# First-loop passes of the expert part by a stage table for each engine

## What is computed

```python
for _ in range(2):
    z_norm = rmsnorm(z, norm_w)                    # z starts as layernorm(x)
    scores = softmax(z_norm @ router_w)            # 8 experts
    topk_vals, topk_idx = top_k(scores, 2)
    topk_vals = topk_vals / (sum(topk_vals) + 1e-9)
    cw = sum(one_hot(topk_idx) * topk_vals)
    mixed = sum over e of cw[:, e] * ((silu(z_norm @ w1[e]) * (z_norm @ w3[e])) @ w2[e])
    z = z + mixed
return x + z
```

## Time and profile before

| | us |
|---|---|
| median of 3 runs (2240.65 to 2243.47) | 2240.81 |
| the profiled execution | 2240.62 |
| its span | 2238.8 |
| expert part: first table operation to the span's end | 1563.1 to 2238.8 |
| tile 0's x transpose | 1584.2 |
| tile 76's | 1748.0 |
| tile 318's | 2193.3 |

### The profile page before, as it was taken

How to read it: one execution, slowest core, us unless ns; L and a number is a source line. 1 busy time by engine, 2 the same in 40 slices (tenths; PEclk the granted TensorE clock), 3 DMA queues, 4 the chain that set the end, 5 groups by cost and what they waited for, 6 DMA issues and landing times. The chain is left out here.

```text
span 2238.8 us, 47085 instructions
## 1 busy us (share of the span) xinstructions
PE 1989.0 (89%) x14589; PEld 951.3 (42%) x14589; DVE 1827.6 (82%) x5158; ACT 1467.0 (66%) x3369; POOL 1234.4 (55%) x1708
## 2 busy tenths in 40 slices
PE   5999999999998899889999999997688999999993
PEld 1222222222222366444444444443355666666662
DVE  8899999999999576788888888888677777767555
ACT  1788888888888623477777777773455655565551
POOL 6253343334321002476767677754767777777776
PEclk9999999999999999799999999997799999999996
DMA  7345335444542002234242433322233444444544
GB/s 188 106 118 144 110 105 139 137 105 122 144 106 87 11 1 57 58 69 106 59 113 61 100 75 87 87 60 64 83 108 112 123 121 119 121 127 124 145 136 114
DMA packets 224625, 226.92 MB, mean 101 GB/s; under 512 B 34049, under 2 KB 187521, under 8 KB 224385
## 3 DMA queue, kind: packets, MB, share of 16 engines
q1 hardware_dynamic: 152432, 164.62, 28.5%
q0 software_dynamic: 16384, 33.59, 5.3%
q10 hardware_dynamic: 55568, 25.71, 4.1%
HBM read 96.48 MB, written 125.76 MB: 99 GB/s over the span
## 5 line engine op out<-in xcount | busy, mean ns | idle before, releaser
L937 ACT ACTIVATE big<-mid_ps 128x512 f32<-128x512 f32 (+2 forms) x1792 | 914.2, 568 | 266.1 <-PE mid_ps L816 258.4
L1022 DVE TENSOR_REDUCE mid_nmax<-mid_ps 128x1 f32<-128x512 f32 (+2 forms) x1280 | 776.4, 657 | 61.3 <-PE mid_ps L795 36.2
L795 PE MATMUL mid_ps<-KT,QT 48*128 48x512 bf16 (+3 forms) x2048 | 604.4, 351 | 68.2 <-DVE mid_nmax L1022 49.6
L816 PE MATMUL mid_ps<-QT,KT 64*128 64x512 bf16 (+3 forms) x2048 | 563.9, 346 | 2.6 <-ACT big L937 2.2
L832 PE MATMUL mid_ps<-big,vv 128*32 128x512 f32 (+3 forms) x4096 | 466.7, 529 | 17.0 <-POOL big L1153 13.3
L795 PEld LDWEIGHTS mid_ps<-KT,QT 48*128 48x128 bf16 x2048 | 158.9, 94 | 585.1 <-DVE mid_nmax L1022 397.3
L1019 DVE CUSTOM_DVE_ANT_0 big<-mid_ps,mask 128x512 bf16<-128x512 f32 (+1 forms) x512 | 304.4, 619 | 68.5 <-PE mid_ps L795 63.7
L1666 PE MATMUL moe_ps<-big,moe_xinT 128*128 x638 | 332.1, 602 | 0.0
L1811 POOL DMA_INDIRECT moe_yg<-rows_out,moe_gat_idx x256 | 250.1, 977 | 85.9 <-issue 65.7
L1797 POOL DMA_INDIRECT rows_in<-moe_xn,moe_scat_idx x240 | 236.2, 984 | 81.2 <-issue 61.3
L1839 DVE TENSOR_TENSOR moe_h<-moe_ps,moe_sg 128x256 f32<-128x256 f32 x319 | 135.0, 423 | 157.3 <-ACT moe_sg L1737 152.6
(11 more groups left out here) (359 smaller groups left out, 3017.7 us busy)
## 6 DMA issues: line engine op xcount, KB each, us to landing
l_spread<-mid_slots SPq DMA_DIRECT2D x128, 384.0 KB, 5.3
rows_in<-mid_blank SPq DMA_DIRECT2D x64, 512.0 KB, 4.4
QT<-l_spread SPq DMA_DIRECT2D x128, 192.0 KB, 4.3
KT<-l_spread SPq DMA_DIRECT2D x128, 192.0 KB, 5.3
moe_xin<-rows_in SPq DMA_DIRECT2D x319, 64.0 KB
rows_out<-moe_y ACTq DMA_DIRECT2D x319, 64.0 KB
x<-in_L_attn_x_dram SPq DMA_DIRECT2D x8, 512.0 KB, 6.9
QT<-mid_mrows SPq DMA_DIRECT2D x256, 6.0 KB
```

The costliest lines, as they stand in the source:

```text
L795: mm = pe.matmul(ps[:, bank, n_keys * a:n_keys * (a + 1)], QT[rows, par, pair, i * P:(i + 1) * P], KT[rows, par, pair, 0:n_keys], start=Tr ...
L816: mm = pe.matmul(ps[:, bank, m * a:m * (a + 1)], KT[rows, own, pair, i * P:(i + 1) * P], QT[rows, own, pair, SEQ - m:SEQ], start=True, sto ...
L937: act.activation(weights_of(r, i, heads), ps[:, ring(S2, n - 2, k), 0:widths[i] * len(heads)], ACT.Exp, scale=scale).then_inc(exp_done, 1)
L1022: dve.tensor_reduce(to, of, X_AXIS, ALU.max, negate=True).then_inc(s1_used, 1)
```

## The change

- `tile_of(k, s, behind)` takes the place of the formula. For passes 1 to 6 (`made(k)`) it reads `AHEAD`, a table for each engine with the distance of each stage from `begin[k]`; tables (s from 21) start 10 steps behind `begin` and go two parts to a step. A stage can't be set ahead of an engine's loop 0. The other passes keep the formula, but ScalarE's stages 5 and 6 of passes 7 to 15 come one loop later.
- `begin` changes for passes 2 to 7 and 9: 2 from -1 to -2, 3 from 8 to 7, 4 from 22 to 18, 5 from 34 to 33, 6 from 46 to 44, 7 from 60 to 56, 9 from 97 to 98.
- The tables of unit 0 (eight parts) are made behind VectorE's stage 5 of pass 1, so behind its z, instead of ahead of everything.
- In `transfers` g8 moves behind s4, and g9 behind s7. Scatters of pass 1 are ready at -8 instead of 0, which lets the first three go without a wait.

Worked out for the passes 2 to 6 with b = `begin[k]`, in loops of each engine:

| stage | before | after |
|---|---|---|
| VectorE z (4) | b+1 | b |
| TensorE transposes (5, 6) | b+4, b+4 | b+2, b+3 |
| ScalarE copies (5, 6) | b+3, b+3 | b+2, b+3 |
| TensorE logits, lT (8, 10) | b+5, b+6 | b+4, b+5 |
| VectorE xn (9, 10) | b+4, b+4 | b+2, b+3 |
| VectorE 12; 13, 14; 15 | b+5; b+6; b+7 | b+5; b+6; b+7 |
| ScalarE exp (15) | b+8 | b+7 |
| TensorE K (16) | b+9 | b+8 |
| VectorE 17, 18 | b+8 | b+9 |
| VectorE 19, 20 | b+9 | b+8 |
| VectorE tables (21 to 28) | b+10 to b+13 | b+10 to b+13 |

```diff
--- before.py
+++ after.py
@@ -1439,18 +1439,31 @@
     HT, MOST = IT * max(sizes), max(tiles_in)
     unit_of = [max(u for u in range(UNITS) if first_of[u] <= k) for k in range(LOOPS * GROUPS)]
     EARLY, PER_TILE = 2, 0.5
-    begin = {2: -1, 3: 8, 4: 22, 5: 34, 6: 46, 7: 60, 8: 76, 9: 97, 10: 117, 11: 137, 12: 158, 13: 179, 14: 200, 15: 224,
+    begin = {2: -2, 3: 7, 4: 18, 5: 33, 6: 44, 7: 56, 8: 76, 9: 98, 10: 117, 11: 137, 12: 158, 13: 179, 14: 200, 15: 224,
              16: 256, 17: 270, 18: 286, 19: 308, 20: 325}
-    transfers = ("s1 s2 s3 g8 s4 s5 s6 g9 s7 g10 s8 g11 s9 g12 s10 g13 s11 g14 s12 g15 s13 g16 s14 g17 s15 g18 "
+    transfers = ("s1 s2 s3 s4 g8 s5 s6 s7 g9 g10 s8 g11 s9 g12 s10 g13 s11 g14 s12 g15 s13 g16 s14 g17 s15 g18 "
                  "g19 g20 g21 g22 g23").split()
 
     def length(k):
 
-        return 10 if k < GROUPS - 1 else 14 if k < GROUPS else 20 if k < LOOPS * GROUPS else 8
-
-    def sides(n):
-
-        return [(k, s) for k, at in begin.items() for s in range(STAGES + TABLES) if at + s * length(k) // STAGES == n]
+        return 14 if k < GROUPS else 20 if k < LOOPS * GROUPS else 8
+
+    ON_PE, ON_ACT, ON_DVE = 2, 1, 0
+    AHEAD = {ON_PE: {5: 0, 6: 1, 8: 2, 10: 3, 16: 6}, ON_ACT: {5: 1, 6: 2, 9: 3, 15: 6},
+             ON_DVE: {4: 0, 9: 2, 10: 3, 12: 5, 13: 6, 14: 6, 15: 7, 19: 8, 20: 8, 17: 9, 18: 9}}
+
+    def tile_of(k, s, behind):
+
+        if made(k) and s < STAGES:
+            return max(begin[k] + AHEAD[behind].get(s, 0), -behind)
+        if made(k):
+            return begin[k] + 10 + (s - STAGES) // 2
+        late = 1 if behind == ON_ACT and s in (5, 6) and routes(k) else 0
+        return begin[k] + s * length(k) // STAGES + late
+
+    def sides(n, behind):
+
+        return [(k, s) for k in begin for s in range(STAGES + TABLES) if tile_of(k, s, behind) == n - behind]
 
     def assigned():
 
@@ -1458,7 +1471,7 @@
         for name in transfers:
             k = int(name[1:])
             if name[0] == "s":
-                ready += [0 if k < EARLY else begin[k] + (STAGES - 1) * length(k) // STAGES + 1] * (2 * IT)
+                ready += [-IT if k < EARLY else tile_of(k, STAGES - 1, ON_DVE) + 1] * (2 * IT)
                 due_at += [base_of[unit_of[k]] - RING] * (2 * IT)
             else:
                 ready += [base_of[unit_of[k - GROUPS] + 1] + LAG + 1] * (2 * IT)
@@ -1472,6 +1485,10 @@
             latest = min(latest, due_at[i])
             spread[i] = min(spread[i], latest)
         return spread
+
+    def made(k):
+
+        return 1 <= k < GROUPS - 1
 
     def routes(k):
 
@@ -1603,7 +1620,7 @@
                     side(k, s)
             for n in range(N + LAG + 1 + behind):
                 tile(n)
-                for k, s in sides(n - behind):
+                for k, s in sides(n, behind):
                     side(k, s)
             for k in range(EARLY + len(begin), SIDES):
                 for s in range(STAGES + TABLES):
@@ -1907,7 +1924,7 @@
                         moments()
                         c.link(dve.tensor_tensor(ms[:, :], mean[:, :], mean[:, :], ALU.mult))
                         c.link(dve.scalar_tensor_tensor(var[:, :], var[:, :], 1e-6, ms[:, :], ALU.add, ALU.add))
-                elif 1 <= k < GROUPS - 1:
+                elif made(k):
                     own = slice(IT * (k - 1), IT * k)
                     if s == 4:
                         c.link(dve.tensor_tensor(zs, xs, each_row(lead.means[:, own]), ALU.subtract))
@@ -1933,17 +1950,19 @@
                     if s == 5:
                         c.link(dve.tensor_tensor(var[:, :], var[:, :], rstd[:, :], ALU.mult))
                         c.link(dve.tensor_scalar(var[:, :], var[:, :], 1e-6, None, ALU.add))
+                if (k, s) == (1, 5):
+                    for part in range(TABLES):
+                        make_tables(0, part)
                 if not routes(k):
                     return
 
-                made = 1 <= k < GROUPS - 1
-                scale = lead.scales[:, IT * (k - 1):IT * k] if made else rstd[:, :]
-                if s == 6 and not made:
+                scale = lead.scales[:, IT * (k - 1):IT * k] if made(k) else rstd[:, :]
+                if s == 6 and not made(k):
                     rsqrt_seed(c, rstd[:, :], var[:, :])
                     cubic_root(c, rstd[:, :], var[:, :], tmp[:, :])
-                if s == 7 and not made:
+                if s == 7 and not made(k):
                     cubic_step(c, rstd[:, :], tmp[:, :])
-                if s == 8 and not made:
+                if s == 8 and not made(k):
                     c.link(newton(c, rstd[:, :], var[:, :], tmp[:, :]))
                 if s in (9, 10):
                     if s == 9 and k >= 3:
@@ -2053,8 +2072,6 @@
                     else:
                         c.link(last)
 
-            for part in range(TABLES):
-                make_tables(0, part)
             run(tile, side, 0)
```

## The result

The changed kernel takes 2258.52 us (2256.32 to 2259.77), the kernel before 2241.56 beside it (2240.65 to 2243.95): a ratio of 1.0072, 95% interval 1.0059 to 1.0085. It is slower, by about 17 us. The forecast of 2241.9 was wrong, and the time lies far outside 2234 to 2247. The profiled execution has a span of 2257.2 us.

A forecast was written before the change was run, and what follows sets the result against it. TensorE, busy 89% of the span, was taken as the bound, made late mostly by VectorE. Terms +1.9 + 1.1 - 2.5 + 1.2 - 0.6 = +1.1 on the median 2240.81 gave 2241.9 us; range 2234 to 2247.

The forecast's parts named there:

- ScalarE's later copies: Second loop, passes 7 to 15: zT copied one loop later, behind the activations, bank free by 0.2 us; priced at nothing.
- late copies: Rival, second loop: the later copies miss by more than 0.2 us, some 0.5 a pass, +4.5, 2246; chance 0.07.
- K of passes 4 to 6: First loop: TensorE's counts wait 1.65 us for VectorE's selb; net +0.66 a pass, +1.9 for the three.
- z wait: First loop: TensorE's first transposes wait 0.9 us for VectorE's z, offset by -0.93 from splitting the transposes; together nothing.
- Tiles 0 to 20: First loop, passes 2 and 3, walked stage by stage: +1.1 us, the least trusted term, between -3 and +4.
- Tables of unit 2 and z of pass 5: First loop: table parts in loops 28 to 31 and z in loop 33 make TensorE lose less; -2.5 us.
- Unit 3's tables and pass 7: First loop, from T(53): VectorE's side work shares five loops, from 54 to 58, instead of seven; +1.2 us.
- Pass 9 at 98: Second loop: one loop between tables and adds gives VectorE up to 1.06 us more; taken as -0.6.
- T(0): Start of tile 0's x transpose, 1584.18 us before; claimed to stay at 1584.2, as it follows SP's first load.
- the rival (2247): First loop: the waits in loops 6, 9 and 15 drop TensorE's clock, likely +5, at most +7.8; chance 0.14.
- the Trainium skill's rule: First loop: short matmul bursts between waits are throttled anew, so each of three waits costs 2.6 us; 2249.
- Shorter distances suffice: Rival, first loop: VectorE is ready earlier, so no waits for K or z; about -7, 2235; chance 0.22.

The follow-up runs named there:

- b3: The kernel before with only ScalarE's stages 5 and 6 of passes 7 to 15 one loop later; 2252.92 us, ratio 1.0053.
- a2: The changed kernel with only ScalarE's stages 5 and 6 of passes 7 to 15 one loop earlier again; 2245.75 us, ratio 1.0019.
- c3: The changed kernel with ScalarE's later copies kept in their loop but set ahead of its store of y; 2246.9 us, ratio 1.0024.
- k1: a2 with TensorE's and ScalarE's stages of passes 2 to 6 one loop later, VectorE's 17 to 20 reordered, pass 7 at 60, pass 9 at 97; 2240.31 us.
- m2: k1 with GpSimd's gathers of pass 9 ahead of the scatters of pass 7 again; 2233.1 us, ratio 0.9965.
- d: a2 with only TensorE's and ScalarE's stages of passes 2 to 6 one loop later; only disturbed runs, 2534.05 to 2544.21 us.
- n: a2 with pass 9's gathers ahead of pass 7's scatters; only disturbed runs, 2530.2 and 2530.08 us, ratios 1.0013 and 1.0019.

## Why the prediction was wrong, step by step

**The step that failed** is the one on ScalarE's later copies, "The copy then ends at T + 1.95 and PE asks for the bank at T + 2.18: free by 0.2", priced at nothing. The term was worth +10.9 by itself (b3) and +13.1 in the changed kernel (311.3 less 298.2 in a2), where the lower clock behind pass 9's wait came on top. Two things were wrong with it. I put the copy behind "the activations" and forgot what else ScalarE's loop issues: the store, with its wait for VectorE's y. And I priced it at nothing with a margin of 0.2, the smallest of the whole working, times eight passes. Without the store the step would have been nearly right (1.3 in all in c3). Its rival stood there, "late copies", with the right sign and place, at 0.5 a pass and 0.07. The price of a miss was taken too low, since the copy was thought to be late by tenths, and not bound to another engine's instruction.

**The first loop** came out as worked out, in kind and nearly in size: 2.8 instead of 1.7. Part of that closeness is luck, as 1.5 of the 2.8 is a drop of the clock that the sum didn't have and that a2's execution of the same tiles hadn't at that place (see the clock below); tiles 0 to 76 took 0.8 more than before in a2.
- *K of passes 4 to 6*: forecast 1.65 of waiting. Measured, pass 4, here in loop 26: T(26) to T(27) takes 3.60 instead of the 1.63 of a free loop.

```profile
1647.32 0.21 PE L1730 MATMUL moe_ps<-moe_selb,lead_upper 128*128 128x72 bf16 x1 [1.52 <-DVE moe_selb L1991]
```

- *z wait*: forecast 0.9 for each of passes 4 to 6; 2.6 in 3 waits from 1620 to 1700 us (a2's row above).
- *Tiles 0 to 20*: forecast +1.1, measured +1.8. The three waits that I forecast in loops 6, 9 and 15 came, with 1.99, 2.40 and 2.42 instead of 2.0, 2.4 and 2.7:

```profile
1599.77 0.21 PE L1730 MATMUL moe_ps<-moe_selb,lead_upper 128*128 128x72 bf16 x1 [1.99 <-DVE moe_selb L1991]
...
1607.07 0.66 PE L1712 MATMUL moe_ps<-ident,big 128*128 128x128 f32 x4 [2.40 <-DVE big L1931]
...
1622.90 0.21 PE L1730 MATMUL moe_ps<-moe_selb,lead_upper 128*128 128x72 bf16 x1 [2.42 <-DVE moe_selb L1991]
```

- *Tables of unit 2 and z of pass 5*: forecast -2.5. T(35) to T(39) shrinks by 4.0 (13.57 in rows 3, now 9.58). The tables now lie ahead of it, in loops 28 to 31, in a stretch (T(20) to T(35)) that also has pass 4's K and grew by 2.4. Together -1.6, where the terms for pass 4 (+0.6) and these give -1.9.
- *Passes 5 and 6*, T(39) to T(53): +1.6, forecast 1.3. *Unit 3's tables and pass 7*, T(53) to T(76): +0.9, forecast +1.2.
- *Pass 9 at 98*: forecast -0.6. a2 has -1.1 and -0.6 in tiles 95 to 102 and 108 to 116, but +0.5 and +1.4 in 102 to 108 and 116 to 123: +0.2.

**T(0)** was to stay at 1584.2 and is 1585.81. The last scatter of pass 0 is issued 0.76 later (1579.60 less 1578.84), as the whole part starts later in that execution; over the seven kernels of the table it is issued between 1578.1 and 1579.6. The other 0.98 is new: the scatter takes 1.94 instead of 0.96, beside VectorE's z of pass 2, which the change moved there:

```profile
1579.46 1.23 DVE L1930 TENSOR_TENSOR big<-x,lead_means 128x1024 f32<-128x1024 f32 x1
1579.60 1.94 POOL L615 DMA_INDIRECT rows_in<-lead_xn,lead_scat  x1 [0.30 <-DVE moe_scat_idx L2013]
...
1583.88 11.42 SPq L1646 DMA_DIRECT2D moe_xin<-rows_in  x11
```

The same issue takes 1.94 in all five kernels with z at that place (after, a2, c3, k1, m2) and 0.96 to 0.97 in the two without it (before, b3). That VectorE's operations make it long is read from this overlap; no run changes that alone. The Trainium skill, GPSIMD Engine Reference, "Key points", says that GpSimd shares its interfaces to SBUF with VectorE and suffers from VectorE's instructions with two SBUF inputs; both operations here have two, and the trace agrees.

**The clock.** I gave 0.14 to the three waits dropping it. In this execution one of the three did: behind the 2.42 of loop 15 two gate matmuls take 1.91 instead of 1.02, at a granted clock of 0.50 (1.2 GHz). The others kept it, and over the 20 tiles the mean is 0.89 against 0.86, as the 3.21 gap of before with its own drop is gone. The length of a wait doesn't decide it. In a2, with the same instructions in these tiles, the 1.95 of loop 6 is followed by the lower clock (0.50 from 1601 to 1603 us), which the z wait of loop 9 then absorbs (0.80 instead of 2.40), and the 2.42 of loop 15 isn't; in c3 both are. T(15) to T(17) takes 7.80 here and 6.13 in a2, so a drop cost 1.7 there, not my 2.6. Two more that I had not named stand in pass 7's part, behind 3.47 us of waiting for y, and behind pass 9's wait for `moe_zT` (the row in b3's section). The stretch behind loop 6's wait, with loop 9's in it, the one behind loop 15's, and the one in pass 7's part (busy time of PE, PEld, DVE, ACT, POOL, then the granted clock), and the wait itself:

```profile
1600.00:1612.00 12.00, 9.61 (x66) 6.35 (x62) 10.06 (x33) 6.73 (x19) 9.14 (x9) 1.00 0.30 87
1624.00:1626.00 2.00, 2.00 (x6) 1.15 (x5) 1.80 (x8) 0.03 (x1) 0.97 (x1) 0.50 0.23 72
1718.00:1722.00 4.00, 3.62 (x12) 2.23 (x12) 3.50 (x17) 1.77 (x6) 3.09 (x4) 0.61 0.26 79
```

```profile
1717.84 0.44 PE L1676 MATMUL moe_ps<-ident,moe_h 128*128 128x128 f32 x2 [3.47 <-DVE moe_y L1865]
```

So the rival (2247) did not come true, though a part of it did. Nor did what I made of the Trainium skill's rule, that every one of the three costs its 2.6 (by the forecast's own sum 2249.7, where I wrote 2249). The case in the Trainium skill, TensorE: Matmul & The Clock Gate, "HAM oscillation — how this bites in real kernels", has waits that are longer than the bursts of matmuls between them. Here the waits of 2.0 to 2.4 stand some 5 and 13 us of work apart, so the rule was stretched.

**"Shorter distances suffice"** (0.22, 2235) was wrong in its mechanism, as the waits show, and couldn't have given 2235 either. With tiles 5.5 us earlier than before, k1 has the same span, as GpSimd's queue is full. The sentence on the queue, "Nothing waits, and what is queued behind them on GpSimd keeps its due steps", failed as well: the scatters of pass 7 wait 9.9 us for their indices in the kernel after, and its queue is 5 us behind from there. In the kernel after that is hidden by the 11.59 at the third-last group, and so wasn't part of the 17 us; in k1 the same idle time took back the whole gain of the tiles.

**Still open** is what each part of k1's edit is worth: TensorE's later stages, pass 7 back at 60, pass 9 back at 97 (d was to tell), and what the order of the transfers is worth in a2 (n). From k1 to m2 it was 7.3 us of span.

## What to carry to other kernels

Before an instruction is moved on an in-order engine, write down everything that this engine issues in the loop, its DMA issues and their waits included, and find who ends the last wait ahead of the new place; a margin of tenths is no cover, and it counts once for every pass. When tiles get earlier and the end doesn't, look for a queue that never pauses, and at its last idle time: from k1 to m2 that went from 9.6 to 2.8 us, and the span was 7.3 shorter. A consumer on the critical engine that would wait is better put a loop later: from a2 to k1 TensorE's waits for `moe_selb` went from 8.9 to 1.2 us.

## What the runs showed of the hardware

- GpSimd, issuing indirect DMAs of 128 rows each, is a bound at 76% busy: 0.97 us each and 0.30 between two, 352 of them in 450 us.
- One such issue took 1.94 us beside VectorE's operation with two inputs in SBUF, in five kernels, and 0.96 in the two that have no such operation there.
- The length of TensorE's wait doesn't tell whether the lower clock follows. It followed a wait of 1.95 (a2) and not one of 1.99 (after); it followed one of 2.42 in the kernel after and not in a2, at the same instruction; and it followed the 2.08 of pass 9 in the kernel after, and not the 2.13 in b3.
